# An attention and gated feed-forward kernel: row block 0's landed halves made in the next pass, and all orders rewritten

## The reference, cut to what matters

```python
xn = _layernorm(x)                       # x: 1 x 1024 tokens x 512, fp32
qkv = xn @ w_qkv.T                       # 32 query heads, 8 key/value heads, 128 wide
scores = einsum('bskgd,btkd->bkgst', qh, kh) * scale
scores = where(causal, scores, min)
probs = softmax(scores)
attn = einsum('bkgst,btkd->bskgd', probs, vh).reshape(1, 1024, 4096)
s = attn @ w_dense.T                     # 1024 x 512
h = relu(s0 * (xn @ (+-1 weights k0))) * 2
h = relu(ei_dense(h, k1, s1)) * 2        # +-1 weights, last fifth of the inputs scaled by -4
g = silu(ei_dense(h, k2, s2))
out = x + s * g
```

## Time and profile before

| | us |
|---|---|
| median of three runs | 943.5 |
| the profiled execution, whole | 943.73 |
| its span, first to last instruction | 941.5 |
| TensorE matmuls busy | 905.5 (96%) |
| VectorE busy | 664.4 (71%) |
| ScalarE busy | 509.4 (54%) |
| GpSimd busy | 464.4 (49%) |
| mean granted TensorE clock | 0.989 |

### The profile page before, as it was taken

One profiled execution on the slowest core, in us unless ns is written; L12 is line 12 of the kernel. 1 busy time (PEld: TensorE's weight loads), 2 busy tenths in 40 slices (PEclk: granted clock), 3 DMA queues, 4 the chain that ended last, 5 costly groups with the idle time before them and its releaser, 6 DMA issues.

```text
span 941.5 us, 15708 instructions
## 1 busy us (share of the span) xinstructions
PE 905.5 (96%) x4272; PEld 761.8 (81%) x4272; DVE 664.4 (71%) x1163; ACT 509.4 (54%) x1077; POOL 464.4 (49%) x372
## 2 busy tenths in 40 slices
PE   7697999999999999999999999999999999999997
PEld 6586887888888788878888888888888788888885
DVE  7464866777666785777667885777677786688853
ACT  3454644646555754655456654656456564555641
POOL 5144534554445553555355463455355453345764
PEclk9998999999999999999999999999999999999999
DMA  6468463876549555675548645686547745455462
GB/s 211 114 181 212 101 144 83 223 187 136 122 109 268 136 122 124 184 207 133 134 112 253 154 114 125 155 236 139 140 104 231 175 112 125 132 153 129 99 171 112
DMA packets 204805, 143.58 MB, mean 152 GB/s; under 512 B 23152, under 2 KB 172144, under 8 KB 204784
## 3 DMA queue, kind: packets, MB, share of 16 engines
q1 hardware_dynamic: 204784, 143.32, 59.1%
HBM read 63.70 MB, written 23.20 MB: 92 GB/s over the span
## 4 chain that ended last, share of the span: by engine, by line
issue 46%; PE 25%; POOL 25%; SPq 1%; DVE 1%; DMA 1%; ACT 1%; POOLq 0%; DVEq 0%
POOL pt_lo L753 17%; POOL w_lo L763 4%; PE ps_m L1094 3%; PE ps_m L1095 3%; PE ps_m L1096 3%; POOL wd_lo L763 3%; PE ps_m L1226 2%; PE ps_o L1094 2%; PE ps_s L1094 2%; PE ps_o L1096 2%; PE ps_o L1095 2%; PE ps_s L1095 2%; PE ps_s L1096 2%; SPq L683 1%; PE ps_s L1211 1%
## 5 line engine op out<-in xcount | busy, mean ns | idle before, releaser
L753 POOL TENSOR_TENSOR pt_lo<-pt_lo,pt_hi 128x512 fp32r<-128x512 f32 x248 | 328.1, 1347 | 397.3 <-ACT pt_hi L841 396.9
L934 DVE CUSTOM_DVE_ANT_0 ps_s<-ps_s,mask 128x32 f32<-128x32 f32 (+31 forms) x256 | 181.5, 714 | 118.9 <-PE ps_s L1096 115.5
L841 ACT ACTIVATE pt_hi<-pt_lo 128x512 fp32r<-128x512 f32 x288 | 169.8, 626 | 116.9 <-DMA pt_lo<-turned 65.5
L1094 PE MATMUL ps_m<-xn_hi,w_hi 128*128 128x512 f32 (+1 forms) x388 | 152.8, 394 | 0.4 <-DVE q_lo L1042 0.4
L1095 PE MATMUL ps_m<-xn_lo,w_hi 128*128 128x512 f32 (+1 forms) x388 | 151.3, 390 | 0.0
L1096 PE MATMUL ps_m<-xn_hi,w_lo 128*128 128x512 f32 (+1 forms) x388 | 151.1, 389 | 0.0
L1094 PE MATMUL ps_s<-k_hi,q_hi 128*128 128x480 f32 (+15 forms) x384 | 128.3, 334 | 9.4 <-ACT prob_odd L805 8.3
L1094 PE MATMUL ps_o<-pt_hi,v_hi 128*128 128x512 f32 x288 | 115.4, 401 | 15.2 <-POOL pt_lo L753 15.2
L1095 PE MATMUL ps_s<-k_lo,q_hi 128*128 128x480 f32 (+15 forms) x384 | 128.6, 335 | 0.0
L1096 PE MATMUL ps_s<-k_hi,q_lo 128*128 128x480 f32 (+15 forms) x384 | 128.2, 334 | 0.0
L805 ACT ACTIVATE prob_odd<-ps_s,small 128x160 f32<-128x160 f32 (+15 forms) x128 | 95.2, 747 | 51.8 <-DVE small L934 50.5
(11 more groups left out here) (99 smaller groups left out, 1414.1 us busy)
## 6 DMA issues: line engine op xcount, KB each, us to landing
inv_rows<-inv SPq DMA_DIRECT2D x64, 256.0 KB, 3.5
pt_lo<-prob_odd SPq DMA_DIRECT2D x128, 128.0 KB, 2.4
pt_lo<-prob_even SPq DMA_DIRECT2D x128, 112.0 KB, 2.3
raw<-wqkv SPq DMA_DIRECT2D x48, 256.0 KB, 3.3
pt_lo<-prob_odd SPq DMA_DIRECT2D x128, 96.0 KB, 2.2
pt_lo<-prob_even SPq DMA_DIRECT2D x128, 80.0 KB, 2.2
raw<-wd SPq DMA_DIRECT2D x32, 256.0 KB, 5.1
turned<-prob_odd SPq DMA_DIRECT2D x32, 256.0 KB, 5.0
```

What stands on the lines that cost most here:

```text
L753: pool.tensor_tensor(pt_lo[:, slot, :], pt_lo[:, slot, :].bitcast(F32), pt_hi[:, hi_slot, :], ALU.subtract).then_inc(land_lo, 1)
L841: act.activation(pt_hi[:, hi_slot, :], pt_lo[:, LAND_AT[i % BLOCKS] + j, :].bitcast(F32), ACT.Copy).then_inc(land_hi, 1)
L934: dve.tensor_tensor_reduce(out=scores, in0=scores, in1=mask[:, S - width(i % BLOCKS, tile):S], scale=-1.0, scalar=BIG, op0=ALU.add, op1=AL ...
L1094: pe.matmul(out, sta_hi, mov_hi, start=start, stop=False)
```

## The change

The two steps `hi.land.8.0` and `lo.land.8.0` leave the ends of the prologue and the loop. In their place `hi.land.0.0` and `lo.land.0.0` stand inside the loop and inside `last`, ahead of the other landings. The code for the index 8 goes away in both engines. All lists of `BODY` and `LAST` are written anew: the same steps, each once, in other places. Among them, in the loop: `load.v` and all four `load.wd` now stand ahead of `dr.3`, `unit.q0.0` has moved from the end to ahead of `weigh.0.0`, `scores.8.3` stands behind `weigh.7.7`, and `hi.land.3.0` to `3.2` stand ahead of `exp.5.1`. In `last`, TensorE runs `final.0` to `final.5` before `weigh.6.0`, VectorE runs `gate.0` to `gate.4` before `mul.weigh.6`, and GpSimd runs `add_x.0` to `add_x.2` before `lo.land.7.3`. No DMA, matmul or elementwise instruction is added or removed, apart from the pair that moves.

```diff
-    act += hi(*values) + hi(("land", first, 0))
+    act += hi(*values)
...
-    pool = lo(*split) + [("zero_odd",)] \
-        + lo(("land", first, 0))
+    pool = lo(*split) + [("zero_odd",)]
...
 BODY = {
     "pe": """
-        scores.1.0 scores.1.1 unit.k.1.0 scores.1.2 scores.1.3 unit.k.1.1 scores.2.0 unit.k.1.2
-        scores.2.1 unit.k.1.3 scores.2.2 unit.q1.1.0 unit.q1.1.1 scores.2.3 scores.3.0 unit.q1.1.2
-        scores.3.1 unit.q1.1.3 unit.q3.1.0 unit.q3.1.1 scores.3.2 unit.q3.1.2 unit.q3.1.3
-        scores.3.3 weigh.0.0 unit.q0.1.0 unit.q0.1.1 unit.q0.1.2 unit.q0.1.3 unit.q2.1.0
-        unit.q2.1.1 unit.q2.1.2 unit.q2.1.3 weigh.1.0 unit.v.1.0 weigh.1.1 scores.4.0 unit.v.1.1
-        scores.4.1 unit.v.1.2 unit.v.1.3 dense.0.0 scores.4.2 scores.4.3 dense.0.1 dense.0.2
...
-        dense.3.0 weigh.4.3 scores.7.0 weigh.4.4 weigh.5.0 scores.7.1 dense.3.1 weigh.5.1
-        dense.3.2 dense.3.3 weigh.5.2 dense.4.0 dense.4.1 scores.7.2 scores.7.3 dense.4.2
-        weigh.5.3 dense.4.3 unit.q2.0.0 unit.q2.0.1 weigh.5.4 unit.q2.0.2 unit.q2.0.3 weigh.5.5
-        unit.k.0.0 unit.k.0.1 weigh.6.6 weigh.6.5 weigh.6.4 unit.k.0.2 unit.k.0.3 unit.q1.0.0
-        unit.q1.0.1 unit.q1.0.2 weigh.6.3 unit.q1.0.3 unit.q0.0.0 unit.q0.0.1 unit.q0.0.2
...
+        scores.1.0 scores.1.1 scores.1.2 unit.q3.1.0 unit.q3.1.1 scores.1.3 unit.q3.1.2 scores.2.0
+        unit.q3.1.3 scores.2.1 unit.k.1.0 unit.k.1.1 unit.k.1.2 scores.2.2 scores.2.3 unit.k.1.3
+        scores.3.0 unit.q0.1.0 unit.q0.1.1 scores.3.1 unit.q0.1.2 scores.3.2 unit.q0.1.3
+        unit.q1.1.0 unit.q1.1.1 unit.q1.1.2 scores.3.3 unit.q1.1.3 unit.q2.1.0 unit.q2.1.1
+        unit.q2.1.2 unit.q2.1.3 unit.q0.0.0 weigh.0.0 unit.q0.0.1 weigh.1.0 scores.4.0 scores.4.1
+        unit.q0.0.2 weigh.1.1 unit.q0.0.3 scores.4.2 scores.4.3 dense.0.0 dense.0.1 dense.0.2
+        dense.0.3 weigh.2.0 scores.5.0 weigh.2.1 weigh.2.2 unit.v.1.0 scores.5.1 unit.v.1.1
+        unit.v.1.2 scores.5.2 unit.v.1.3 dense.1.0 scores.5.3 dense.1.1 weigh.3.0 dense.1.2
...
+        scores.7.1 unit.q3.0.0 unit.q3.0.1 unit.q3.0.2 unit.q3.0.3 dense.3.0 weigh.5.1 weigh.5.2
+        scores.7.2 dense.3.1 scores.7.3 weigh.5.3 dense.3.2 dense.3.3 unit.k.0.0 weigh.5.4
+        unit.k.0.1 unit.k.0.2 weigh.5.5 unit.k.0.3 weigh.6.6 weigh.6.5 weigh.6.4 dense.4.0
+        dense.4.1 dense.4.2 dense.4.3 unit.q2.0.0 unit.q2.0.1 unit.q2.0.2 unit.q2.0.3 dense.5.0
+        dense.5.1 weigh.6.3 dense.5.2 dense.5.3 weigh.6.2 unit.v.0.0 weigh.6.1 weigh.6.0
+        scores.8.0 unit.v.0.1 unit.v.0.2 unit.v.0.3 weigh.7.0 weigh.7.1 weigh.7.2 scores.8.1
...
     "act": """
-        hi.split.wd0 hi.split.wd1 hi.split.wd2 exp.1.0 exp.1.1 exp.1.2 exp.1.3 exp.2.0 exp.2.1
-        hi.unit.k.1 hi.split.wd3 exp.2.2 exp.2.3 hi.unit.q1.1 exp.3.0 exp.3.1 hi.unit.q3.1 exp.3.2
-        hi.land.1.0 hi.land.1.1 exp.3.3 hi.weigh.0 hi.unit.q0.1 hi.split.q0 hi.split.q1
-        hi.unit.q2.1 hi.split.q2 hi.split.q3 hi.split.k hi.land.2.0 hi.land.2.1 exp.4.0
...
-        hi.weigh.6 exp.8.2 exp.8.3 hi.land.7.4 hi.land.7.5 hi.land.7.6 hi.land.7.7 hi.vblocks.0
-        hi.weigh.7 hi.land.8.0
+        hi.split.wd0 hi.split.wd1 hi.split.wd2 exp.1.0 exp.1.1 exp.1.2 exp.1.3 hi.split.wd3
+        exp.2.0 hi.unit.q3.1 exp.2.1 exp.2.2 hi.unit.k.1 exp.2.3 hi.land.0.0 exp.3.0 hi.unit.q0.1
+        hi.split.q0 exp.3.1 exp.3.2 hi.land.1.0 hi.unit.q1.1 exp.3.3 hi.land.1.1 hi.split.q1
+        hi.unit.q2.1 hi.split.q2 hi.split.q3 hi.split.k hi.weigh.0 exp.4.0 hi.land.2.0 exp.4.1
+        hi.land.2.1 hi.land.2.2 exp.4.2 hi.unit.q0.0 exp.4.3 hi.weigh.1 exp.5.0 hi.land.3.0
+        hi.land.3.1 hi.land.3.2 exp.5.1 hi.land.3.3 exp.5.2 hi.split.v hi.weigh.2 exp.5.3
...
+        hi.weigh.6 hi.land.7.4 hi.land.7.5 hi.land.7.6 exp.8.0 hi.land.7.7 exp.8.1 exp.8.2
+        hi.vblocks.0 hi.weigh.7 exp.8.3
     "dve": """
-        max.1.0 max.1.1 max.1.2 max.1.3 max.2.0 max.2.1 flip.1 max.2.2 lo.unit.k.1 max.2.3
-        inverse.1 max.3.0 max.3.1 flip.2 lo.unit.q1.1 max.3.2 inverse.2 max.3.3 lo.unit.q3.1
-        mul.weigh.0 flip.3 lo.unit.q0.1 lo.weigh.0 lo.unit.q2.1 inverse.3 mul.weigh.1 max.4.0
...
-        mul.weigh.6 max.8.3 lo.land.7.1 lo.unit.v.0 lo.weigh.6 flip.8 lo.land.7.4 lo.dense.5
-        inverse.8 lo.land.7.7 lo.vblocks.0 mul.weigh.7 lo.weigh.7 lo.dense.6 lo.dense.7
+        max.1.0 max.1.1 max.1.2 max.1.3 max.2.0 flip.1 max.2.1 inverse.1 lo.unit.q3.1 max.2.2
+        max.2.3 max.3.0 lo.unit.k.1 flip.2 max.3.1 max.3.2 lo.unit.q0.1 inverse.2 max.3.3
+        lo.unit.q1.1 flip.3 lo.unit.q2.1 mul.weigh.0 inverse.3 max.4.0 max.4.1 lo.weigh.0 max.4.2
+        max.4.3 mul.weigh.1 lo.unit.q0.0 lo.dense.0 flip.4.0 lo.weigh.1 max.5.0 flip.4.1 flip.4.2
...
+        lo.unit.v.0 lo.weigh.6 lo.land.7.4 max.8.1 max.8.2 lo.land.7.7 lo.vblocks.0 mul.weigh.7
+        max.8.3 lo.weigh.7 flip.8 lo.dense.6 inverse.8 lo.dense.7
     "pool": """
-        lo.split.wd0 lo.split.wd1 lo.split.wd2 lo.split.wd3 lo.land.1.0 lo.land.1.1 lo.split.q0
-        lo.split.q1 lo.split.q2 lo.split.q3 lo.land.2.0 lo.land.2.1 lo.land.2.2 lo.split.k
-        lo.split.v lo.land.3.0 lo.land.3.1 lo.land.3.2 lo.land.3.3 lo.land.4.0 lo.land.4.1
...
-        lo.land.7.0 lo.land.7.2 lo.land.7.3 lo.land.7.5 lo.land.7.6 lo.land.8.0
+        lo.split.wd0 lo.split.wd1 lo.split.wd2 lo.split.wd3 lo.land.0.0 lo.split.q0 lo.land.1.0
+        lo.land.1.1 lo.split.q1 lo.split.q2 lo.split.q3 lo.split.k lo.land.2.0 lo.land.2.1
+        lo.land.2.2 lo.land.3.0 lo.land.3.1 lo.land.3.2 lo.land.3.3 lo.split.v lo.land.4.0
...
+        lo.land.6.0 lo.land.7.0 lo.land.7.2 lo.land.7.3 lo.land.7.5 lo.land.7.6
     "sp": """
-        load.q0 load.q1 load.q2 load.q3 dw.1 rw.1 load.k dr.1 dw.2 rw.2 rr.1 dr.2 dw.3 load.v rw.3
-        rr.2 load.wd0 load.wd1 load.wd2 dr.3 load.wd3 move.4.0 move.4.1 move.4.2 move.4.3 rr.3
...
+        load.q0 load.q1 load.q2 load.q3 dw.1 rw.1 load.k dr.1 dw.2 rw.2 load.v dr.2 dw.3 rr.1
+        load.wd0 load.wd1 load.wd2 load.wd3 rw.3 dr.3 rr.2 move.4.0 move.4.1 move.4.2 move.4.3
...
 LAST = {
     "pe": """
-        scores.1.0 scores.1.1 unit.q1.1.0 scores.1.2 scores.1.3 unit.q1.1.1 scores.2.0 scores.2.1
-        unit.q1.1.2 unit.q1.1.3 scores.2.2 scores.2.3 unit.q3.1.0 scores.3.0 unit.q3.1.1
-        unit.q3.1.2 unit.q3.1.3 unit.q0.1.0 scores.3.1 unit.q0.1.1 unit.q0.1.2 scores.3.2
-        unit.q0.1.3 unit.q2.1.0 unit.q2.1.1 unit.q2.1.2 unit.q2.1.3 scores.3.3 unit.k.1.0
...
-        hidden.1.1.0.0 hidden.1.1.0.1 hidden.1.1.0.2 hidden.1.1.0.3 hidden.1.1.1.0 hidden.1.1.1.1
-        hidden.1.1.1.2 hidden.1.1.1.3 hidden.1.1.2.0 hidden.1.1.2.1 hidden.1.1.2.2 hidden.1.1.2.3
-        hidden.1.1.3.0 weigh.6.2 hidden.1.1.3.1 hidden.1.1.3.2 hidden.1.1.3.3 weigh.6.1 final.0
-        weigh.6.0 dense.5.0 final.1 dense.5.1 weigh.7.0 weigh.7.1 dense.5.2 final.2 weigh.7.2
-        weigh.7.3 dense.5.3 final.3 weigh.7.4 weigh.7.5 weigh.7.6 dense.6.0 final.4 weigh.7.7
-        final.5 final.6 final.7 dense.6.1 dense.6.2 dense.6.3 dense.7.0 dense.7.1 dense.7.2
-        dense.7.3
+        scores.1.0 scores.1.1 scores.1.2 unit.q3.1.0 scores.1.3 unit.q3.1.1 scores.2.0 scores.2.1
+        unit.q3.1.2 unit.q3.1.3 scores.2.2 unit.q2.1.0 unit.q2.1.1 scores.2.3 unit.q2.1.2
+        scores.3.0 unit.q2.1.3 scores.3.1 unit.q1.1.0 scores.3.2 scores.3.3 unit.q1.1.1
+        unit.q1.1.2 unit.q1.1.3 unit.k.1.0 unit.k.1.1 unit.k.1.2 unit.k.1.3 weigh.0.0 unit.q0.1.0
...
+        weigh.6.6 weigh.6.5 hidden.1.1.0.0 hidden.1.1.0.1 hidden.1.1.0.2 hidden.1.1.0.3
+        hidden.1.1.1.0 hidden.1.1.1.1 hidden.1.1.1.2 weigh.6.4 hidden.1.1.1.3 weigh.6.3
+        hidden.1.1.2.0 weigh.6.2 hidden.1.1.2.1 hidden.1.1.2.2 hidden.1.1.2.3 hidden.1.1.3.0
+        hidden.1.1.3.1 hidden.1.1.3.2 hidden.1.1.3.3 final.0 final.1 weigh.6.1 final.2 final.3
+        final.4 final.5 weigh.6.0 weigh.7.0 weigh.7.1 dense.5.0 dense.5.1 weigh.7.2 weigh.7.3
+        dense.5.2 weigh.7.4 weigh.7.5 dense.5.3 final.6 weigh.7.6 weigh.7.7 dense.6.0 final.7
+        dense.6.1 dense.6.2 dense.6.3 dense.7.0 dense.7.1 dense.7.2 dense.7.3
     "dve": """
...
-        lo.hidden.1.1.2 lo.hidden.1.1.3 lo.land.7.1 mul.weigh.6 gate.0 lo.weigh.6 gate.1
-        lo.land.7.4 gate.2 lo.land.7.7 lo.dense.5 gate.3 mul.weigh.7 gate.4 lo.weigh.7 gate.5
-        lo.dense.6 gate.6 lo.dense.7 gate.7 add_x.7
...
+        mul.weigh.5 lo.dense.4 lo.weigh.5 lo.land.6.1 lo.hidden.1.1.0 lo.hidden.1.1.1
+        lo.hidden.1.1.2 lo.hidden.1.1.3 gate.0 gate.1 lo.land.7.1 gate.2 gate.3 gate.4 mul.weigh.6
+        lo.land.7.4 lo.weigh.6 lo.land.7.7 lo.dense.5 gate.5 mul.weigh.7 lo.weigh.7 lo.dense.6
+        gate.6 lo.dense.7 gate.7 add_x.7
     "pool": """
...
-        low.hidden.0.1.0 low.hidden.0.1.1 lo.land.6.6 lo.land.6.5 low.hidden.0.1.2 lo.land.6.3
-        low.hidden.0.1.3 lo.land.6.2 lo.land.6.0 low.hidden.1.1.0 low.hidden.1.1.1
-        low.hidden.1.1.2 low.hidden.1.1.3 lo.land.7.0 lo.land.7.2 lo.land.7.3 add_x.0 add_x.1
-        lo.land.7.5 lo.land.7.6 add_x.2 add_x.3 add_x.4 add_x.5 add_x.6
...
```

(14 more changed lines are left out.)

142 lines of the change are left out of this document (67 added, 75 removed).

## The result

The changed kernel took 977.04 us (median of four runs, 971.92 to 983.36) against 945.37 us for the kernel before (942.27 to 948.25, four runs). The ratio is 1.034, 95% interval 1.026 to 1.041: slower, where I had forecast 929.5 us. The profiled execution took 979.07 us with a span of 977.0 us; by my sum its span should have been 927.3. So 49.7 us are to be found.

A forecast was written before the change was run, and what follows sets the result against it. TensorE was taken as the bound, so reordering wins only its waits. From 943.7 us, pass 0 gains 16.4, passes 1 to 6 gain 6.7 and pass 7 loses 8.9: 929.5 us, range 918 to 939.

The forecast's parts named there:

- Pass 0, the step removed: Pass 0: ScalarE's 7.06 us idle goes; of TensorE's 8.30 us wait at `scores.2.0`, 0.3 us stays.
- Pass 0, the rest: Pass 0: new waits of 1.0 us for `unit.q0.0` and `scores.4.0`, 1.0 at `weigh.3.0`, 0.8 for the clock; pass 109.2 us.
- the step that failed: Every pass: `dr.3` lands between 1 us later and 2 us earlier; `exp.5.1` costed at nothing, bound 0 to 1 us.
- The slower rival: `dr.3` behind four weight loads: each us landed beyond 35.9 holds `exp.5.1` and `scores.5.3`, costing 7 us; chance 0.06.
- `weigh.7.0`: Passes 0 to 6: TensorE waits 0.85 us for row block 7's moves and low half, a chain of 14.8 us.
- My one rival for this wait: At `weigh.7.0`: row block 7 lands in time because SP's issue time shortens; part of a case of chance 0.16.
- The clock: Half speed behind long TensorE waits: 0.8 us in pass 0, 2.0 us in the last pass, no term for the loop.
- The last pass: Pass 7: TensorE waits 9.0 us before `weigh.7.3` behind GpSimd's x additions, clock 2.0 us; 8.9 us longer in sum.
- No new waits in the loop: Rival: row block 7 lands in time and pass 0 is clean, about 920 us; chance 0.16.
- the last pass does not wait: Rival, pass 7: x load comes early or the additions do not hold `lo.land.7.3`, 918.5 us; chance 0.08.
- the jam stays: Rival: `weigh.3.0` in pass 0 waits 4 us again, or `scores.5.3` 0.5 us each pass; 934 to 939 us; chance 0.15.

The follow-up runs named there:

- a1: The kernel before with only the landed halves of row block 0 moved into the next pass, all other orders kept: 931.39 us against 939.92, ratio 0.993.
- b1: The changed kernel with `dr.3` ahead of `rw.3` in SP's loop list: 954.56 us, ratio 1.018 to the kernel before.
- c1: The changed kernel with `add_x.0` to `add_x.2` behind `lo.land.7.3`, 7.5 and 7.6 in GpSimd's last list: 955.19 us, ratio 1.015 to the kernel before.
- e2b: The changed kernel with the edits of b1 and c1 together: 941.21 us against 941.3 for the kernel before, ratio 1.001.
- f1b: e2b with `rr.6` behind all moves of row block 7 and `mul.weigh.6` two steps later in VectorE's loop list: 931.16 us, ratio 0.989 to the kernel before.
- i1: f1b with `exp.4.1` ahead of `hi.land.2.0` in ScalarE's loop list: 929.99 us, ratio 0.986 to the kernel before.
- g1b: a1 with `weigh.5.5` behind `unit.k.0.0` and `unit.k.0.1` in TensorE's loop list, so `rr.6` goes out closer to the moves: 937.16 us, ratio 0.998 to the kernel before.
- d1: The changed kernel with `rr.6` behind the first eight of row block 7's sixteen DMAs in SP's loop list: 987.53 us, ratio 1.050 to the kernel before.

## Why the prediction was wrong, point by point

**Pass 0, the step removed: right.** The 7 us of idle ScalarE went, and a1 shows the pass 11.3 us shorter from the moved landing alone.

**Pass 0, the rest: right places, too small.** I had 1.0 us for `unit.q0.0` and `scores.4.0`, from ScalarE reaching `land.1.0` 18.0 us into the pass. It got there at 56.67 - 35.18 = 21.5:

```profile
52.84 0.61 ACT L803 ACTIVATE prob_odd<-ps_s,small 128x416 f32<-128x416 f32 x1 [6.67 <-DMA turned<-prob_odd]
...
54.80 0.50 PE L1092 MATMUL ps_m<-xn_hi,w_hi 128*128 128x512 f32 x1 [2.44 <-DVE q_lo L1040]
...
56.67 0.63 ACT L839 ACTIVATE pt_hi<-pt_lo 128x512 fp32r<-128x512 f32 x1 [0.87 <-DMA pt_lo<-turned]
```

The first row is the reason: `exp.3.0` writes where `dw.1` reads, and ScalarE idles 6.67 us until that write to DRAM is through. `dw.1` went out 9.8 us into the pass, near the 9.2 that I had; I did not ask who waits for it. Behind `exp.3.0` stands `hi.unit.q0.1`. So TensorE waited for a low half of q (2.6 us at 54.80), then 2.5 us at `scores.4.3`, 1.1 at `weigh.5.0` and 2.1 at `weigh.7.0`. The 1.0 us at `weigh.3.0` didn't come, though `dr.3` went out at 36.6 us and not at 27 to 29: it took 6.9 us and not 10.8 to land, and TensorE came later itself. For the clock I had 0.8; three stretches at half clock cost 10.1 us busy / 2 = 5.1. Together (2.6 - 1.0) + 2.5 + 1.1 + (2.1 - 0.85) + (5.1 - 0.8) - 1.0 = 9.8, against 9.3 measured.

**`dr.3`: the step that failed.** "I put its landing between 1 us later and 2 us earlier" and "I cost it at nothing" are the sentences. It landed 1.6 to 4.5 us later than before, and `exp.5.1` held `scores.5.3` for 14.9 us over passes 1 to 6. The size of the effect was foreseen, even its price: each us past 35.9 costs one us in each pass; ScalarE got the data at 38.7 in pass 4 and TensorE lost 2.5. What I got wrong is what `dr.3` stands behind. I looked at the steps that it is moved past (`load.wd3`, `rw.3`) as issue time, 0.5 us each, and at the loads' wait for GpSimd. I did not ask what `rw.3` itself waits for, and whether the change had moved that too. It had: `rr.1`, which now stands five steps ahead of `rw.3`. The wait in question is quoted nowhere in my text, though the line stands in the function that I read for the x loads. The slower rival had the right place and price, at 0.06, and named the wrong step ahead: b1 keeps four loads ahead of `dr.3` and the wait is gone. The price held there too: with landings at 35.5 to 36.9 us `scores.5.3` hardly waits.

**`weigh.7.0`: right place, mis-sized.** 0.85 us forecast, 2.1 to 2.5 measured in passes 1 to 6, 13.9 in all against 5.1. I had taken the 10.68 us of issue and the landing behind it as fixed, since nothing between `weigh.6.4` and GpSimd had been changed. The neighbour ahead of the chain had: `weigh.5.5`, which `rr.6` hangs on, now stands closer to `weigh.6.4`. The trace of before couldn't price that, since it has one distance only (1.7 us). My one rival for this wait was that the moves get faster, and I had none for slower ones.

**`scores.4.3` and `scores.5.2`: not seen.** 4.1 us over passes 1 to 6, `exp.4.1` behind `hi.land.2.0`.

**The clock: the multiplier that I left out of the loop.** Six stretches at half clock lie in passes 1 to 6, with TensorE busy throughout: 20.5 us busy, 10.3 us lost, more than the 8.8 us that `weigh.7.0` cost beyond the forecast. I had priced the clock where I had seen it, behind 8.3 and 5.4 us of waiting, and in the loop at nothing. The trace of before already had a stretch in the loop that I left out, in pass 1, behind 1.67 us of idle:

```profile
199.07 0.50 PE L1094 MATMUL ps_o<-pt_hi,v_hi 128*128 128x512 f32 x1 [1.67 <-POOL pt_lo L753]
...
200.20:203.60 3.40, 3.40 (x12) 3.40 (x13) 0.99 (x2) 1.32 (x4) 2.52 (x3) 0.50 0.58 131
```

It also had 2.19 us of idle in pass 3 with none behind it. The runs show the same: the clock falls behind much shorter waits than 5.4 us, in some passes and not in others: in the changed kernel behind five of seven waits at `weigh.7.0` and, in the two other passes, behind `scores.5.3`; in b1, with the same waits at `weigh.7.0`, behind four of seven. Over the span it goes roughly as the waits go: the granted clock is 0.979 in the changed kernel, 0.986 in b1, 0.987 in c1, 0.995 in e2b, 0.994 in f1b (where two thirds of the half clock lie in the prologue), 0.998 in i1. The Trainium skill ("TensorE: Matmul & The Clock Gate", Terms) takes half of the throttled time as the penalty. For the short stretches, busy throughout, the trace agrees (3.40 of 3.40 us busy). For the one at the end of pass 7 it doesn't: 10.20 us throttled, 3.02 us busy, so 1.5 us lost and not 5.1.

These four terms sum to 14.9 + 8.8 + 4.1 + 10.3 = 38.1 us for passes 1 to 6, against 36.8 off the forecast.

**The last pass: right.** 9.0 us of wait forecast, 9.46 of idle measured (9.6 from start to start); 2.0 us forecast for the clock, 1.5 measured; from the issue of the x loads to the first addition it was 951.71 - 946.88 = 4.8 us (5.1 forecast). The 2.6 us that follow from the Trainium skill ("DMA: Bandwidth & Descriptors", Anatomy of one DMA) would have been too short again: here seven loads and `rr.7` are in flight together. 2.9 us came from three small waits earlier in the pass that I had not looked for.

**The rivals.** "No new waits in the loop" and "the last pass does not wait" were wrong, "the jam stays" had the wait at `scores.5.3` in it at 0.5 us a pass. With all gains on one side and a slower case of 0.06, the chances treated a rewrite of every list as one known edit with small doubts, where the lists have up to 150 steps and any one of them can stand behind the wrong wait.

**Still open.** Whether the backlog behind `rr` is made by its bytes (256 KB), its write to all 128 partitions or its reading from one small place in DRAM wasn't tried. The Trainium skill ("DMA: Bandwidth & Descriptors", Queues, rings and completion order) says that SP owns one ring on each DMA engine; that fits a transfer that waits behind the one issued ahead of it, but no run here separates the rings. What makes the clock fall behind one wait of 2.4 us and not behind the next is open too. So are the 4.5 us by which the loop of i1 is above the forecast.

## What to carry to other kernels

When steps move in a strict list, write down for every step that another one now stands behind what it waits for, and whether that releaser moved as well: the cost sat two hops away (`rr.1`, `rw.3`, `dr.3`, `exp.5.1`, `scores.5.3`). Put transfers whose data are due ahead of those that wait for a slow landing, and keep a large spreading read from going out right ahead of a stream of transfers that is on the path (1.7 us ahead cost nothing here, 0.8 us did). Where one engine is the bound, count each new wait of 2 us as up to 3.7, since the clock may fall behind it; and try the one edit with a plain reason by itself before a rewritten order.

## What the runs showed of the hardware that I had not expected

- A 256 KB `inv_rows` read issued less than 1 us ahead of a stream of 128 KB moves lengthens every one of 16 moves, not only the first: 2.4 us each with 1.7 us between or with the read behind them (before, a1, f1b), 2.9 to 3.4 with 0.6 to 0.8 us (after, e2b, g1b), 3.6 to 3.9 behind a read in the middle of the stream (d1); medians of passes 1 to 6.
- Half clock, 1.2 GHz in place of 2.4, behind idle times of TensorE of 1.9 to 3.5 us: nine stretches in the changed kernel, and a tenth with the 9.46 us. Outside the prologue there are five in b1, three in e2b, one in f1b and none in i1.
- The landing of the 256 KB `rr.1` took 5.5 to 8.4 us in passes 1 to 6 with four 256 KB loads issued behind it, and 3.3 to 3.7 us at its old place, without them.
